# Graph network kernel: stage one's first 24 tiles gathered raw into a ring of 24, and the input's layer norm done by pairs of groups

## The reference

```python
h = jnp.maximum(_layernorm(x), 0.0)
# three SAGE layers: mean over the incoming edges, two 128x128 products, leaky relu 0.01
agg = segment_sum(h[src], dst, N) * inv_deg
h = leaky_relu(agg @ Wl.T + b + h @ Wr.T, 0.01)
x = x + h_after_three_layers
h = jnp.maximum(_layernorm(x), 0.0)
# one attention layer: softmax over the incoming edges
e = leaky_relu(a_s[src] + a_d[dst], 0.2)
x = x + segment_sum((h @ W)[src] * softmax_by_dst(e), dst, N) + bias
```

## Time and profile before

| | |
|---|---|
| time, median of 3 runs | 2746.61 us (2743.92 to 2747.4) |
| profiled execution, its own time | 2745.45 us |
| its span, first to last instruction | 2743.7 us |
| busy in the span | DVE 1976.4 us (72%), PE 1880.6 (69%), POOL 1645.0 (60%), ACT 1277.1 (47%) |
| mean granted TensorE clock | 0.942 |
| moved by DMA | 552.66 MB, 201 GB/s over the span |

### The profile page before, as it was taken

How to read it: one execution, slowest core, us unless ns; L and a number is a source line. 1 busy time by engine, 2 the same in 40 slices (tenths; PEclk the granted TensorE clock), 3 DMA queues, 4 the chain that set the end, 5 groups by cost and what they waited for, 6 DMA issues and landing times. The chain is left out here.

```text
span 2743.7 us, 45000 instructions
## 1 busy us (share of the span) xinstructions
PE 1880.6 (69%) x10632; PEld 1465.7 (53%) x10632; DVE 1976.4 (72%) x7624; ACT 1277.1 (47%) x3317; POOL 1645.0 (60%) x1944
## 2 busy tenths in 40 slices
PE   0005788888784889988894777777776465565655
PEld 0003555555553666666663666666665455465555
DVE  7986455545553777777784888888885688888888
ACT  4894333333330111111111566666666677777776
POOL 5575666666636666666645666666663566666663
PEclk9999999999996999999997999999997799989898
DMA  6785777777774777777773777777776466666665
GB/s 216 275 303 162 219 220 219 219 223 219 218 216 117 218 217 224 220 212 224 215 214 116 207 214 215 215 214 215 215 216 169 125 168 180 171 175 173 174 173 153
DMA packets 617784, 552.66 MB, mean 201 GB/s; under 512 B 75377, under 2 KB 578391, under 8 KB 617488
## 3 DMA queue, kind: packets, MB, share of 16 engines
q1 hardware_dynamic: 374064, 311.88, 38.6%
q0 software_dynamic: 52160, 108.53, 16.4%
q10 hardware_dynamic: 191296, 129.32, 14.6%
HBM read 342.48 MB, written 207.75 MB: 201 GB/s over the span
## 5 line engine op out<-in xcount | busy, mean ns | idle before, releaser
L703 POOL DMA_INDIRECT rows<-tab,idx x1190 | 1134.9, 954 | 716.4 <-issue 308.7
L703 POOL DMA_INDIRECT rows<-tab_c,idx x401 | 381.3, 951 | 271.0 <-issue 96.5
L807 ACT ACTIVATE sage<-bank,b_low 128x512 f32<-128x512 f32 x196 | 134.3, 685 | 706.8 <-remote 201.6
L1392 DVE TENSOR_SCALAR mask<-iota,dcol 128x256 f32<-128x256 f32 (+1 forms) x1203 | 405.8, 366 | 0.3
L945 PE MATMUL bank<-mask,rows 128*128 128x256 f32 (+1 forms) x1960 | 393.3, 350 | 13.4 <-DMA rows<-tab,idx 11.9
L945 PEld LDWEIGHTS bank<-mask,rows 128*128 128x128 f32 x1960 | 345.9, 197 | 57.4 <-issue 15.1
L1411 DVE TENSOR_TENSOR bank<-bank,sage 128x512 f32<-128x512 f32 x196 | 136.0, 694 | 330.9 <-issue 321.1
L1053 PE MATMUL bank<-ident,mask 128*128 128x128 f32 x784 | 148.2, 319 | 201.9 <-issue 147.6
L971 PE MATMUL bank<-sage,wcat 128*128 128x512 f32 x392 | 210.6, 619 | 82.4 <-DVE sage L1424 66.6
L1063 PE MATMUL bank<-rows,sage 128*128 128x131 f32 x1568 | 238.4, 301 | 3.5 <-issue 1.9
L1020 PEld LDWEIGHTS bank<-rows,mask 128*128 128x128 f32 x1568 | 211.9, 197 | 46.0 <-issue 37.4
(11 more groups left out here) (229 smaller groups left out, 3509.7 us busy)
## 6 DMA issues: line engine op xcount, KB each, us to landing
sage<-inv_d SPq DMA_DIRECT2D x392, 128.0 KB
turned<-sage ACTq DMA_DIRECT2D x392, 128.0 KB
tab<-sage ACTq DMA_DIRECT2D x392, 128.0 KB
sage<-turned SPq DMA_DIRECT2D x392, 128.0 KB
tab_c<-sage ACTq DMA_DIRECT2D x196, 132.0 KB
own_w<-tab_c SPq DMA_DIRECT2D x196, 132.0 KB
tab<-sage SPq DMA_DIRECT2D x49, 512.0 KB, 3.2
xin<-tab SPq DMA_DIRECT2D x196, 128.0 KB
```

Source lines behind the costliest of these rows:

```text
L703: eng.indirect_dma_start(out=rows[:, s.win[w], 0:width], out_offset=None, in_=table, in_offset=bass.IndirectOffsetOnAxis(ap=idx[:, s.w + w ...
L1392: m = eng.tensor_scalar(to[:, g.mw[w], a:b], io[:, a:b], node, None, ALU.is_equal)
```

## The change

Three things are done together.

1. The ring of windows has 24 tiles in place of 12 (DEEP = 24). SOON is now 24: POOL fetches the windows of the first 24 tiles (49 windows) from raw x, before it waits for the table. Of these, four tiles at a time (a chunk; nine windows in the first, eight in the others) are normalised in place: `raw_stats` and `raw_shift` on DVE, `raw_scale` and `raw_norm` on ACT. Chunk 0 comes before stage one; chunk c + 1 is worked on in stage one, at the steps of tiles 4c and following. In stages two and three POOL may still run only 12 tiles ahead (LEAD), and the attention uses a ring of 12 (CDEEP) as before. The memset of the ring (L594) is gone, and scratch tiles of the preparation now lie inside the ring.
2. The layer norm of the input goes by pairs of groups: POOL's moments, the square root, and the scale and shift are one instruction for two groups. The root of pair k comes ahead of the normalising of pair k - 1, and DVE forms the scale and shift of pair k - 1 after the bn_stats of pair k's second group. The seven buffers, SP's loop and the eight normalising instructions of each group are as before.
3. In the index work, nine sums over a row that were an instruction of their own (tensor_reduce) are taken along by the instruction before them (accum_out).

```diff
-WRING = UNROLL // SG * SW
+CRING = UNROLL // SG * SW
+WRING = 2 * CRING
-DEEP = 12
+DEEP = 24
+LEAD = (None, DEEP, 12, 12)
+CDEEP = 12
-SOON = 6
+SOON = WG
+CHUNKS = SOON // SG
...
-            eng.memset(rows[:, :, :], 0.0).then_inc(S["zrow"], 1)
...
             def moments(a, b):
-                for g in range(a, b):
+                for g in range(a // 2 * 2, b - b % 2 + (b == NSG), 2):
+                    n = min(2, NSG - g)
                     r = g % LNR
-                    of = st_g[:, r, :, :]
+                    of = st_g[:, r:r + n, :, :]
-                    eng.wait_ge(S["bn_v"], g + 1)
+                    eng.wait_ge(S["bn_v"], g + n)
...
             for t in range(SOON):
                 s = Step(None, t)
+                if group < NSG:
+                    moments(group, min(group + 2, NSG))
+                    group += 2
                 for w in s.new:
-                    if group < NSG:
-                        moments(group, group + 1)
-                        group += 1
                     eng.indirect_dma_start(out=rows[:, s.win[w], 0:D], out_offset=None, in_=x,
...
-                        wait(eng, S["agg_done"], ka + s.t - DEEP + 1)
+                        wait(eng, S["agg_done"], ka + s.t - LEAD[ph] + 1 if s.t >= LEAD[ph] else 0)
...
-            for g in range(NSG + 1):
-                if g == GAHEAD:
+            for g in range(0, NSG + 2, 2):
+                if g == 6:
                     weights()
-                if g < NSG:
-                    eng.wait_ge(S["ln_v"], 3 * (g + 1))
-                    eng.activation(std_g[:, g % LNR, :], half_m[:, g % LNR, :], ACT.Sqrt, ...
-                o = g - 1
-                if o >= 0:
+                n = min(2, NSG - g)
+                if n > 0:
+                    r = g % LNR
+                    eng.wait_ge(S["ln_v"], 3 * (g + n))
+                    eng.activation(std_g[:, r:r + n, :], half_m[:, r:r + n, :], ACT.Sqrt, ...
+                for o in range(max(g - 2, 0), min(g, NSG)):
                     eng.wait_ge(S["nmr_v"], o + 1)
                     for j in range(GJ):
                         a = eng.activation(x_g[:, o % GR, j * D:(j + 1) * D], ...
...
+            raw_scale(0)
+            for t in range(SG):
+                raw_norm(Step(None, t))
...
                 def phase(s):
+                    if ph == 1 and s.k == 0 and s.t < SOON - SG:
+                        raw_scale(s.t // SG + 1)
+                    o = s.at(2)
+                    if ph == 1 and SG <= o.t < SOON:
+                        raw_norm(o)
...
-                    if g >= BEHIND:
-                        shift_g(g - BEHIND)
+                    if g >= BEHIND + 1 and g % 2 == 1:
+                        shift_g(g - BEHIND - 1)
...
-            op(eng.tensor_tensor(cmp_n[:, :], d_nat[:, :], d_nxt[:, :], ALU.is_gt))
-            op(eng.tensor_reduce(stat[0:NAT_P, 0:1], cmp_n[:, :], AX.X, ALU.add))
+            op(eng.scalar_tensor_tensor(cmp_n[:, :], d_nat[:, :], 0.0, d_nxt[:, :], ALU.add, ALU.is_gt,
+                                        accum_out=stat[0:NAT_P, 0:1]))
...
-            for g in range(NSG - BEHIND, NSG):
+            for g in (NSG - BEHIND - 1, NSG - 1):
                 shift_g(g)
...
+            raw_stats(0)
+            close_up(ends, MOVES_S - 2)
+            raw_shift(0)
+            close_up(ends, MOVES_S - 1)
...
+                    if ph == 1 and s.t < SOON - SG:
+                        if s.k == 0:
+                            raw_stats(s.t // SG + 1)
+                        if s.k == 1:
+                            raw_shift(s.t // SG + 1)
```

More of the change, by code:

```diff
@@ L76, in __init__ @@
         self.q = off % DEEP
+        self.c = off % CDEEP
         self.n = off % NRING
@@ L86, in __init__ @@
         self.win = [(own + n) % WRING for n in range(NW)]
+        self.cw = [(own + n) % CRING for n in range(NW)]
         self.mw = [(own + n) % MRING for n in range(NW)]
@@ L120, in ahead, with gathered, chunk @@
     return [s.at(k) for k in range(d + 1)] if s.i is None and s.t == 0 else [s.at(d)]
-def gathered(q, n):
-    return sum(NW - (t % WG > 0) for t in range(q, n, DEEP))
+def gathered(q, n, ring=DEEP):
+    return sum(NW - (t % WG > 0) for t in range(q, n, ring))
+def chunk(c):
+    a, b = ((SG * k) * 2 + (k > 0) for k in (c, c + 1))
+    return a, b
 def columns(g, w):
@@ L411, in build @@
         general += [f"gn_{n}{k}" for k in range(LAYERS + 2) for n in ("ld", "st")]
-        main = [f"{n}{k}" for n, ring in (("ol", OWN), ("sq", OWN), ("il", RING), ("cl", RING)) for k in range(ring)]
+        main = [f"{n}{k}" for n, ring in (("ol", OWN), ("sq", OWN), ("il", RING), ("cx", 4)) for k in range(ring)]
         general += ["ge_v", "ge_a", "ge_m", "gn_v", "gn_a", "gn_m"]
@@ L870, in phase_c @@
                         a, b = columns(s, w)
-                        m = eng.activation(score[:, s.mw[w], a:b], cut[:, s.win[w], a:b], ACT.Identity,
+                        m = eng.activation(score[:, s.mw[w], a:b], cut[:, s.cw[w], a:b], ACT.Identity,
                                            bias=rows[:, s.win[w], D:D + 1])
@@ L890, in phase_c @@
                         a, b = part_columns(o.k, w)
-                        m = eng.activation(prob[:, o.mw[w], a:b], cut[:, o.win[w], a:b], ACT.Exp,
+                        m = eng.activation(prob[:, o.mw[w], a:b], cut[:, o.cw[w], a:b], ACT.Exp,
                                            bias=ed[:, o.g, 2 * o.k + w:2 * o.k + w + 1])
@@ L1359, in fast_vector @@
             op(eng.tensor_scalar(b_low[:, :], b_col[:, :], 0.01, None, ALU.mult))
[L1360 removed]
+            for b in range(AT["moves"], MOVES_S - 2):
                 close_up(ends, b)
[L1362 to L1377 removed]
+            def raw_stats(c):
+                for t in range(SG * c, SG * c + SG):
+                    s = Step(None, t)
+                    rows_there(eng, s, 1)
+                    for w in s.new:
+                        m = eng.bn_stats(st_f[:, s.w + w, :], rows[:, s.win[w], 0:D])
+                op(m)
+                for w in range(*chunk(c)):
+                    m = eng.bn_aggr(mv_f[:, w, :], st_f[:, w, :])
+                m.then_inc(S["ln_v"], 1)
+            def raw_shift(c):
[3 more added lines that the diff above has]
+                eng.wait_ge(S["rs_v"], NSG + c + 1)
+                eng.scalar_tensor_tensor(nmr_f[:, a:b], mv_f[:, a:b, 0], -1.0, rstd_f[:, a:b], ALU.mult, ALU.mult
+                                         ).then_inc(S["nmr_v"], 1)
+            raw_stats(0)
+            close_up(ends, MOVES_S - 2)
+            raw_shift(0)
+            close_up(ends, MOVES_S - 1)
             op(eng.tensor_copy(deg[:, :, 0:1], ends[:, :, 0:1]))
@@ L1526, in cut_part @@
                         if w == 0:
-                            wait(eng, S["pr_a"], g.t - DEEP + 1)
+                            wait(eng, S["pr_a"], g.t - CDEEP + 1)
                         masks(g, cut, iota_b, "cut_v", w, -CUT)
@@ L1538, in phase_c @@
                         f = s.at(n - SG)
-                        eng.wait_ge(S[f"cl{f.q}"], 16 * (f.uses(DEEP) + 1))
-                    q0 = s.at(-SG).q
+                        loaded, before = cut_ld[f.c]
+                        eng.wait_ge(loaded, 16 * (before + f.uses(CDEEP) + 1))
+                    q0 = s.at(-SG).c
                     oc = own_c[:, q0:q0 + SG, :, :].rearrange("p r j c -> p (r j) c")
```

156 lines of the change are left out of this document (71 added, 85 removed).

## The result

| | before | changed |
|---|---|---|
| median of the runs, us | 2747.01 (4 runs, 2743.92 to 2748.28) | 2800.92 (4 runs, 2798.14 to 2803.03) |
| ratio, 95% interval | | 1.0201 (1.0188 to 1.0213) |
| profiled execution, its span, us | 2745.45, 2743.7 | 2803.03, 2801.3 |
| DVE released from the layer norm, us | 212.9 | 242.6 |
| sums of the first, second, third pair, us | 235.24, 242.50, 248.07 | 269.81, 273.81, 309.96 |

Slower, as forecast, but by 54 us where 14 were forecast (2761); the interval of the ratio is clear of 1. The loss stands at two places, and both lie before 310 us. The layer norm ends 29.7 us later. Then stage one makes the sums of two pairs and stops for 34 us. The stretches show it: busy times of PE, weight loads, DVE, ACT and POOL, granted clock, DMA share, GB/s.

A forecast was written before the change was run, and what follows sets the result against it. No single bound: DVE, then ACT in the norm, transfer traffic in stage one. Norm +18.8, fewer windows -1.1, POOL's lead -4, chunks +2 make +15.7 on 2745.45: 2761 us, range 2736 to 2778.

The forecast's parts named there:

- Part 1's mechanism: Layer norm by pairs: seven buffers too few, so ACT waits 2.7 us in a loop of load, bn_stats, moments and root.
- the rival that loads come back sooner: Layer norm: loads take 4.3 us for 5.25, DVE free at 209.5, total 2739 or 2736; chance 0.22.
- the 15.7 of the sum: Whole kernel: 18.8 - 1.1 - 4 + 2 us, added to the profiled execution's 2745.45.
- Sizes in part 1: Layer norm by pairs: DVE free at 231.7 for 212.9 before, +18.8 us; +6.1 at the floor step, +22.2 at the upper.
- The start: Layer norm: group 7's load lands at 52 to 53.5, and pair 2 starts at 55.5.
- The step: Layer norm, time per pair: 8.5 us for 17 pairs during index work, 7.75 for the last 4.
- The sums taken along: Index work on DVE: nine reduces, about 8 us, cost nothing at best when fused; counted as no gain on the span.
- Part 2, from release to first sums: Before stage one: 9 raw windows for 13 on the chain to the first sums, -1.1 us.
- Part 2, POOL's lead: Stage one: some 11 windows leave the traffic-bound time, some by skipped ring stops, -4 us; ends 0 and -10.
- The chunks in the stage: Stage one: 40 raw windows normalised on ACT and DVE, mostly in idle time, +2 us; from 0 to 27.
- the rival that they bite: Stage one: each of five chunks holds ACT and DVE 2 to 3 us, another +10, total 2771; chance 0.16.
- the 6.07 us a pair against 4.36 without windows: Stage one: time per pair with and without POOL's windows, read as transfer traffic bounding the stage, about 1.7 us a pair.

The follow-up runs named there:

- numbers 1 and 4: The kernel before with only the norm by pairs: ratio 1.0121; the changed kernel with nine norm buffers for seven, loads issued two groups further ahead: 1.0085.
- number 2: The changed kernel with moments, roots and shifts of single groups again, the rest of the change kept: ratio to before 1.0094.
- Numbers 5 and 6: Single groups, four raw tiles normalised in one go, no chunk in stage one; POOL waits for sums 24 tiles back (1.0104) or 12 back (1.0008).
- number 3: The changed kernel with POOL waiting for the sums 12 tiles back from the 13th raw tile on and through stage one: ratio to before 1.0139.
- Number 10: The kernel before with fused sums, nine norm buffers, and POOL's landing pauses after the 4th, 8th and 12th tile of stages two and three: 0.9981.
- Number 7: The kernel before with PE's stage-one transposes reporting once for two tiles, 4 semaphore updates a pair for 6: ratio 1.0016.
- numbers 9 to 11: number 9, Number 10, and a third: number 9's kernel with the same landing pause also for the next 24 tiles from the table, ratio to before 1.0067.
- the ring alone: Ring of 24, single groups, four raw tiles normalised before stage one, no chunk in it, POOL waiting for the sums 24 tiles back: ratio 1.0104.
- number 9: The changed kernel with nine norm buffers, and POOL waiting after every fourth raw tile until its own windows have landed: ratio to before 1.0047.

## Why the prediction was off

**Where it was right.** Part 1's mechanism: the seven buffers, with the root moved ahead, close a loop of load, bn_stats, moments and root that ACT must wait for. The turn of the loop shown above has its terms, and numbers 1 and 4 show that it is this that ends the norm late: pairs alone bring the late end, two more buffers take it away. The landing of the loads, on which one rival hung, was 5.25 us there and 5.0 in the median over 52 to 205 us, so the rival that loads come back sooner is out. By the Trainium skill, page "SBUF — State Buffer", section "The DMA setup-cost knee", it would be an estimate of 3.2 us; the trace disagrees again.

**Where the 42 us are missing.** The span grew by 57.6 us for the 15.7 of the sum. Of the 41.9 between them 10.9 lie in the norm, 6.0 between its end and the first sums, and 25 behind the first sums.

**Sizes in part 1.** DVE was to be released at 231.7 and is at 242.6: +29.7 for +18.8. Two terms were too small. The start: group 7's load was put at 52 to 53.5; DVE gets to that group at 56.76, after 9.72 us of idle for the load, its moments are stretched (58.48 to 61.93), and pair 2 is normalised from 62.24 on, not 55.5 (+6.7). The step: 21 of them take 179.6 us, 8.55 each for a mean of 8.36 (+4.1). The first 17 took 8.64 each for 8.5, the last four 8.17 for 7.75. These four are a long one with a wait and a short one without in turn, as the sum had it (10.52, 6.37, 9.43 and 6.37 from 209.13 on, for 9.1 and 6.4), and index work still lies between the groups then (DVE's L1279 at 229.52).

**The sums taken along** cost the op, as long as it was before (L1205: 0.97 us for 0.99), and 0.08 us for the read of the accumulator, so the best end was nearly the right one. Only the two of L1196 pay more: the op before was a tensor_scalar of 0.64 us, and with the sum it takes 1.05. With single groups, number 2 has DVE released 3.6 us earlier than before; with pairs the gain hides in the loop, as argued.

**Part 2, from release to first sums: 27.2 us for 21.2.** The step "on the chain to the first sums there are 9 windows in place of 13" forgot chunk 1. DVE takes it right behind the masks (265.05 to 267.35), and ACT's root of it stands in the queue ahead of the first own rows: ACT idle for 7.80 us until 267.39. Some 5 of the 6 us are that, an estimate: the masks are there at 265.12, and the sums begin at 269.81.

**Part 2, POOL's lead: the step that failed.** "Nor does POOL stop for the ring of 12 in the first 25 us", counted as part of -4 us. POOL's stops are what lets PE's updates through; without them the stage all but stands still until POOL itself comes to a wait. From the first sums to the end the change was to give 2 us back and it cost 23 (57.6 of span, 34.6 of it there at the first sums). Numbers 5 and 6 size the unbroken gathers alone at 25 us. The chunks in the stage, +2, and the rival that they bite, +10, were about the wrong thing: number 3 has all of them and no stop.

Behind it lies a misreading of the pace. I took the 6.07 us a pair against 4.36 without windows for traffic. But POOL issues eight windows at 1.25, stops for some 2 us until PE's sums are reported, and so on: 12 us for two pairs. The 2.32 us before 239.62 were such a stop, and I priced it as a loss to be saved. Number 10 fits this: with POOL's issuing as the pace, a TensorE that is ahead gains nothing.

Ring, rows and windows behaved as forecast in one thing: the last window of stage one is issued 62 us before stage two's first (some 70 were forecast), where before it was 36. The lead was really taken and really given back.

**What stays open.** Whether PE's work is late or only its report, and what in a gather holds it. A row's end can't tell: by the Trainium skill, page "Perfetto Trace Analysis", section "Summary: the profiler window per engine type", the end of a TensorE row is an estimate, and the way of the semaphore update isn't in it. The trace agrees as far as it goes, with an end at 275.72 and a release at 303.92. That PE, which takes its matmuls in order, has those of the next step on record from 288.02 on, 16 us ahead of that release, speaks for a late report; the products of number 10 that come singly speak for late work. Both may be so. Number 7 excludes only that the number of updates matters in runs of eight gathers. Nor does a run tell POOL's issuing from the transfers that it has in flight: the pauses of numbers 9 to 11 end both.

## What to carry to other kernels

Before a wait is taken out of an engine that issues transfers, look in the trace for a place where it already runs without that wait (here the start of stage two) and read what the others do in that time. A wait that looks like lost time can be what lets another engine's updates through. And if instructions are merged over two groups, count the buffers of the loop anew: two more made the pairs as fast as single groups, and single groups a little faster too (last roots at 205.42, 208.61 and 206.17).

## What the runs showed of the hardware that was not expected

While POOL issues gathers back to back (1.25 us each), those who wait for TensorE's semaphore updates go on late, by up to 28 us in the changed kernel and 42 with the ring alone (247.05 to 289.38). Early in a run updates still pass at once (239.30 to 239.33 with the ring alone, after 15 gathers); later they come one by one, 5.5 to 17.6 us apart (250.18 to 289.38). The rest come a while after POOL's last gather, in the main longer after longer runs. POOL's own idle time until it goes on: some 2 us after 8 gathers (1.86 before 885.57 in the kernel before), 4.52 after 25, 5.05 after 29, 5.46 after 33, 5.29 after some 43, 7.37 after 49. ACT's update reached TensorE within 0.14 us in the same stretch. TensorE's own matmuls, with no wait between them, came 1.4 to 2.8 us apart at the end of such a run in number 10 (883.49 to 889.80). A pause of 2 to 3 us for the landing of POOL's own gathers, after each eight or so, was enough to let the updates through (number 9, up to 282.16).
